# A fused patch, fast-weight attention and mixture-of-experts kernel: the down weights of the experts are loaded and split before the attention loop instead of in it

## The reference

```python
h = patch_norm_linear(x)                      # 32 images, 36 patches each, 3840 features -> 192
h = concatenate([h, txt], axis=1)             # 32 x 164 tokens of 192
n = layernorm(h)
# fast weights: k0, v0, g0 come from batch 0 alone
retrieved[t] = q[t] @ fw[t];  fw[t+1] = 0.95 * fw[t] + 0.1 * g0[t] * outer(k0[t], v0[t])   # per head, 8 heads of 64
h = h + n + retrieved @ w_out.T
n = layernorm(h);  xf = rms_norm(n, norm_w)
probs = softmax(xf @ router_w.T);  comb = probs * one_hot(top_k(probs, 2))               # 8 experts
y = einsum(silu(xf @ gate_w[e].T) * (xf @ up_w[e].T) * comb[:, e], down_w[e])             # 384 hidden
out = h + n + y
```

## Time and profile before

| | |
|---|---|
| time, median of three runs | 548.85 us (548.56 to 549.72) |
| the profiled execution: span | 547.2 us; the page gives no other time of this execution |
| busy: TensorE / weight loads / VectorE / ScalarE / GpSimd | 89% / 84% / 69% / 56% / 35% |
| mean granted TensorE clock | 0.962 of full |
| head, attention loop, experts | up to 111 us, 111 to 224 us, 236 to 547 us |

### The profile page before, as it was taken

One profiled execution on the slowest core, in us unless ns is written; L12 is line 12 of the kernel. 1 busy time (PEld: TensorE's weight loads), 2 busy tenths in 40 slices (PEclk: granted clock), 3 DMA queues, 4 the chain that ended last, 5 costly groups with the idle time before them and its releaser, 6 DMA issues.

```text
span 547.2 us, 12568 instructions
## 1 busy us (share of the span) xinstructions
PE 484.7 (89%) x3157; PEld 461.4 (84%) x3158; DVE 375.3 (69%) x1293; ACT 304.8 (56%) x773; POOL 192.3 (35%) x272
## 2 busy tenths in 40 slices
PE   2999998998798987789999999999999999999900
PEld 2999997887576876789999999999999999999800
DVE  4969996459789879848566566565565565565597
ACT  5485967449578876435444444444444444444473
POOL 1000000006577777733333333333433433433330
PEclk9999999999799989799999999999999999999965
DMA  8988214711433342542222222222222222235897
GB/s 322 415 331 350 63 53 130 283 38 51 120 94 110 101 126 76 139 117 73 71 76 76 68 79 73 68 82 70 68 83 69 69 83 68 68 84 145 273 353 223
DMA packets 62463, 71.67 MB, mean 131 GB/s; under 512 B 19057, under 2 KB 56626, under 8 KB 61410
## 3 DMA queue, kind: packets, MB, share of 16 engines
q1 hardware_dynamic: 49920, 51.43, 30.6%
q0 software_dynamic: 8208, 16.95, 8.7%
q10 hardware_dynamic: 4306, 2.95, 1.8%
HBM read 49.43 MB, written 21.86 MB: 130 GB/s over the span
## 4 chain that ended last, share of the span: by engine, by line
PE 71%; DVE 15%; DMA 6%; ACT 4%; issue 2%; ACTq 1%; SPq 0%; POOL 0%; DVEq 0%; POOLq 0%
PE bank L838 8%; PE pair L838 6%; PE bank L1088 5%; PE bank L1084 5%; PE bank L1087 5%; PE bank L1086 5%; PE bank L1085 5%; PE bank L1095 5%; PE pair L1104 4%; PE bank L1104 4%; PE pair L1073 3%; PE pair L983 3%; ACT yall L749 2%; PE pair L987 2%; PE pair L1106 2%
## 5 line engine op out<-in xcount | busy, mean ns | idle before, releaser
L782 POOL DMA_INDIRECT disp<-xf,posu x82 | 85.0, 1037 | 151.0 <-ACT xf L654 123.8
L1575 DVE TENSOR_TENSOR hh<-sg,bank 128x384 f32<-128x384 f32 x89 | 49.3, 554 | 99.5 <-ACT sg L730 99.5
L812 POOL DMA_INDIRECT ydram<-ysb,dnow x89 | 88.5, 994 | 69.4 <-DMA ydram<-ysb,dnow 35.1
L730 ACT ACTIVATE sg<-bank 128x384 f32<-128x384 f32 x89 | 43.7, 492 | 116.8 <-PE bank L1088 116.8
L1084 PE MATMUL bank<-wa,xh 128*128 x178 | 67.5, 379 | 0.0
L1088 PE MATMUL bank<-wa,xl 128*128 x178 | 60.4, 339 | 0.0
L1087 PE MATMUL bank<-wa,xh 128*128 x178 | 59.9, 337 | 0.0
L1085 PE MATMUL bank<-wa,xh 128*128 x178 | 59.7, 336 | 0.0
L1086 PE MATMUL bank<-wa,xl 128*128 x178 | 59.7, 335 | 0.0
L809 POOL COPY dnow<-dest 128x1 uint32 (+1 forms) x89 | 16.9, 190 | 114.2 <-DVE ysb L1585 104.8
L838 PE MATMUL bank<-wcT,imgT 128*128 128x193 f32 x240 | 41.7, 335 | 10.6 <-DMA imgT<-in_pixels 10.6
(11 more groups left out here) (262 smaller groups left out, 1171.2 us busy)
## 6 DMA issues: line engine op xcount, KB each, us to landing
xs<-disp SPq DMA_DIRECT2D x89, 96.0 KB, 2.0
band<-in_bands SPq DMA_DIRECT2D x4, 1536.0 KB, 12.1
yall<-ydram SPq DMA_DIRECT2D x7, 768.0 KB, 7.8
imgT<-in_pixels SPq DMA_DIRECT2D x4, 768.0 KB, 12.5
imgT<-in_pixels SPq DMA_DIRECT2D x2, 1536.0 KB, 16.0
hres<-in_text SPq DMA_DIRECT2D x1, 3072.0 KB, 25.5
wa<-in_gate_up_w SPq DMA_DIRECT2D x8, 384.0 KB, 8.5
ring<-in_gate_up_w SPq DMA_DIRECT2D x32, 96.0 KB
```

Of the source, the lines that this page charges most:

```text
L782: pool.indirect_dma_start(disp, bass.IndirectOffsetOnAxis(ap=posu[c % XBUF][:, 2 * j + k:2 * j + k + 1], axis=0), xfd[c % XBUF][:, j, :], None
L812: pool.indirect_dma_start(ydram, bass.IndirectOffsetOnAxis(ap=dnow[b][:], axis=0), ysb[r][:], None).then_inc(s_ys[b], 16)
```

## The change

The load of the down weights moves up in SP's order, behind that of the attention weights and behind a wait for the row sums. Units 0 to 3 leave the loop: `down_high` and `down_low` do them at four places of the head in ScalarE and three in VectorE (two pieces at one of them). `turn_units` deals only the other 24 units over the same 19 turns.

```diff
         def turn_units(t):
 
-            return range(min(t, TURNS) * UNITS // TURNS, min(t + 1, TURNS) * UNITS // TURNS)
+            n = UNITS - DOWN_UNITS
+            return range(DOWN_UNITS + min(t, TURNS) * n // TURNS, DOWN_UNITS + min(t + 1, TURNS) * n // TURNS)
...
                     sp.dma_start(aw[:], attn_w).then_inc(s_attw, 16)
+                    sp.wait_ge(s_red, 2)
+                    sp.dma_start(wd4[:, :, 1, :].bitcast(F32), down_w).then_inc(s_rawd, 16)
 
             sp.wait_ge(s_sq, 30)
             sp.wait_ge(s_pat, PTILES)
-            sp.dma_start(wd4[:, :, 1, :].bitcast(F32), down_w).then_inc(s_rawd, 16)
...
+            def down_high(n):
+                if n == 0:
+                    act.wait_ge(s_rawd, 16)
+                g = slice(6 * n, 6 * n + 6)
+                nc.scalar.copy(wd4[:, g, 0, :], wd4[:, g, 1, :].bitcast(F32)).then_inc(s_hi, 1)
...
                     for n in range(4):
                         projection(n)
                     add_norm(3, slice(4, 8))
+                    down_high(0)
...
             add_norm(4)
+            down_high(1)
+            down_high(2)
             act.wait_ge(s_k0, 5)
...
             add_norm(5)
+            down_high(3)
             act.wait_ge(s_gs, 1)
...
+            def down_low(n):
+                v.wait_ge(s_hi, n + 1)
+                raw = wd4[:, 6 * n:6 * n + 6, 1, :]
+                v.tensor_tensor(raw, raw.bitcast(F32), wd4[:, 6 * n:6 * n + 6, 0, :].bitcast(F32), ALU.subtract
+                                ).then_inc(s_lo, 1)
...
             for h in range(4):
                 vals(h)
+            down_low(0)
+            down_low(1)
             v.wait_ge(s_k0, 6)
...
             v.tensor_tensor(kgate[:], kgate[:], cst[:, C_KEY:C_KEY + CHUNKS], ALU.mult).then_inc(s_kgr, 1)
+            down_low(2)
...
             v.memset(bank[4][0:DH, 0:2 * XC], 0.0).then_inc(s_st0, 1)
+            down_low(3)
             st.wait()
```

More of the change, by code:

```diff
@@ L379, in unit @@
             k = n - DOWN_UNITS
-            return None if k < 0 else (k // 3, k % 3)
+            return k // 3, k % 3
         def turn_units(t):
-            return range(min(t, TURNS) * UNITS // TURNS, min(t + 1, TURNS) * UNITS // TURNS)
+            n = UNITS - DOWN_UNITS
+            return range(DOWN_UNITS + min(t, TURNS) * n // TURNS, DOWN_UNITS + min(t + 1, TURNS) * n // TURNS)
         def load_results(eng, g):
@@ L666, in high @@
             def high(n):
[L667 to L671, removed]
-                else:
[L673 to L680, removed]
+                e, k = unit(n)
+                if k == 0:
+                    act.wait_ge(s_rawm[e], 16)
+                    ins = nc.scalar.activation(wa5[:, e, 0], wa5[:, e, 1].bitcast(F32), ACT.Copy, scale=nwab[:, 0:1])
+                else:
+                    r = 2 * e + k - 1
+                    act.wait_ge(s_rawr[r % RING], 32 * (r // RING + 1))
+                    ins = nc.scalar.activation(wa5[:, e, 2, k - 1], ring[r % RING][:], ACT.Copy, scale=nwab[:, 1:2])
                 ins.then_inc(s_hi, 1)
@@ L1435, in low @@
                 v.wait_ge(s_hi, n + 1)
-                if unit(n) is None:
-                    raw = wd4[:, 6 * n:6 * n + 6, 1, :]
-                    ins = v.tensor_tensor(raw, raw.bitcast(F32), wd4[:, 6 * n:6 * n + 6, 0, :].bitcast(F32), ALU.subtract)
-                else:
[L1440 to L1448, removed]
+                e, k = unit(n)
+                if k == 0:
+                    raw = wa5[:, e, 1]
+                    ins = v.scalar_tensor_tensor(out=raw, in0=raw.bitcast(F32), scalar=nwab[:, 0:1],
+                                                 in1=wa5[:, e, 0].bitcast(F32), op0=ALU.mult, op1=ALU.subtract)
+                else:
+                    both = wa5[64:P, e, 2, k - 1, :]
+                    ins = v.scalar_tensor_tensor(out=both, in0=ring[(2 * e + k - 1) % RING][64:P, :], scalar=nwab[64:P, 1:2],
+                                                 in1=both.bitcast(F32), op0=ALU.mult, op1=ALU.subtract)
                 ins.then_inc(s_lo, 1)
```

## The result

| | before | changed |
|---|---|---|
| time, median | 549.29 us (548.56 to 550.14, 4 runs) | 544.91 us (543.73 to 545.99, 4 runs) |
| ratio, 95% interval | | 0.9921 (0.9902 to 0.9941) |
| profiled execution | span 547.2 us | span 544.2 us, own time 545.99 us |
| mean granted TensorE clock | 0.962 | 0.969 |

The forecast was 544.6 us. Two later sets of runs of the changed kernel, each beside the kernel before on its chip, gave 545.22 us (541.67 to 548.46, 12 runs; 0.9919, 0.9895 to 0.9944) and 544.38 us (542.31 to 544.59, 6 runs; 0.9919, 0.9896 to 0.9942). The gain is 4.4 us. Of the times further down one, e7's of 553.67 us, is a slow execution, which the ratios leave out.

What follows compares the result with a forecast made beforehand. It took VectorE and TensorE taking turns in the attention loop as the bound, with GpSimd's scatter queue as second chain. 0.2 + 0.3 + 2.0 + 1.7 = 4.2 us off the 548.85 us median gave 544.6 us, range 542.2 to 547.4.

Steps and rivals of the forecast that it cites:

- Transfer: Down load on SyncE's queue, moved behind the attention weights: lands near 61 us in a 10 us hole, gains nothing.
- Head: Four down pieces placed in idle time of ScalarE and VectorE before the loop: cost nothing.
- The rival of a load in the way: SyncE's queue at 64.78: the down load delays the fourth band, making the kernel slower, up to 551.1 us; chance 0.05.
- Before residual 1: Loop, VectorE: a rest piece replaces a down piece ahead of these residuals; saves 0 to 0.7 us, taken as 0.2.
- ScalarE's deviations: Loop, chunk 1: ScalarE casts fewer down pieces, so VectorE's 0.28 us wait for the deviations goes; saves 0.3 us.
- the row of pieces: VectorE before residual 2, from 133.09 us: pieces in a row shrink from 4.78 to 2.82 us; saves 2.0 us.
- The clock: TensorE's half-clock falls in chunks 3 and 8: one of two goes, at the dear price; saves 1.7 us, between 0 and 4.7.
- GpSimd's cap: GpSimd's scatter queue in the loop allows 3.2 to 9.6 us of gain, likely 5.5; binds only where no fall comes.
- my sign of being wrong: Loop's end: the prediction is wrong if GpSimd's last loop scatter moves less than the mask of chunk 10.
- The stretches: Scatters on GpSimd lengthened beyond their regular steps, 6.3 us in all; estimated to shrink to 4 us.
- The hole at the experts' start: TensorE idles between fillers and first expert slot as VectorE outgains GpSimd; a fall there costs 1.7 to 3.0 us; chance 0.08.
- the rival of no fall: Loop: both clock falls go, 7.2 us on VectorE's chain, cut to about 6 by GpSimd, 542.9 us; chance 0.22.

Runs made afterwards that it cites:

- e7: Changed kernel with 4 filler products on TensorE ahead of each mask wait from chunk 2 on; 546.19 us, ratio 0.9912 to the kernel before.
- e1: Kernel before with only the down load moved behind the attention weights, all splits still in the loop; 550.02 us, ratio 1.0012.
- e3: Changed kernel with ScalarE's casts in the head but VectorE's four down subtractions back in the loop; 548.75 us, ratio 0.9981.
- e4: Changed kernel with the 24 remaining units at the turns they had among 28; 546.48 us, ratio 0.9946.
- e9: Kernel before with 4 filler products ahead of each mask from chunk 2 on; 550.45 us, ratio 1.0007.
- a0_after: The changed kernel run again, unaltered, beside the kernel before; 545.22 us over 12 runs, ratio 0.9919.
- r_e8: Changed kernel with 4 fillers ahead of each mask from chunk 2 on and 54 instead of 40 before the experts; 543.83 us, ratio 0.9915.
- r_after: The changed kernel run again, unaltered, on the same chip as r_e8; 544.38 us over 6 runs, ratio 0.9919.
- e2: Changed kernel with each head piece done twice on ScalarE and VectorE; 552.51 us, ratio 1.0064.

## Why the prediction was right, and which of its terms were not

**Transfer, nothing: right** (e1). Its size was off: I took 410 GB/s, and once the down load ran alone it moved at 325 to 353, so it landed at 62.9 and not 61. That left 2.9 us to the band's issue.

**Head, nothing: right**, with the waits left that I had worked out, to 0.2 us. The rival of a load in the way, my only slower one, has nothing for it.

**Before residual 1, 0.2 us: zero.** Mask 0 to mask 2 is 19.46 before and 19.45 after. VectorE waits 0.56 us for TensorE at 126.95. The measured value is the lower bound of my 0 to 0.7; I should have taken it, since I had written that TensorE leads there.

**ScalarE's deviations, 0.3 us, and the row of pieces, 2.0 us: 0.46 and 2.1.** Together 2.56 for my 2.3, and e3 separates them. e4 shows why it is no more than that.

**The clock, 1.7 us: this is the term that was mis-sized.** I had one of two falls stay "at the dear price". The dear one went, mask 3 to mask 4 fell from 12.99 to 9.90 us, a gain of 3.1; the cheap one stayed at its price (mask 4 to mask 10: 59.8 and 59.7 us). Against the profile before, the loop gained 2.56 + 3.1 + 0.1 = 5.8 us, not 4.2. But the profile before was not typical. In e1, e3 and e9, where the pieces' row still stands, the fall behind mask 3 holds 3.4 us and not 6.9, so that mask 3 to mask 4 is 11.45 to 11.57 us and the fall costs 1.5 to 1.7; and the late fall does not come (mask 4 to mask 10: 58.2 to 58.3 us). The changed kernel's three profiles have the late one and not the first. Either side then has one fall of 3.4 us, the clock term is about nothing, and on VectorE's chain, mask 0 to mask 10, 101.6 to 102.1 us stand against 99.3 to 99.7: 1.9 to 2.7 us, the pieces and little more.

The medians lie 4.4 us apart all the same, and the ledger shows where the rest can be. In e1, e3 and e9 GpSimd's queue leads at the loop's end: it stood still for 3.16 to 3.28 us behind chunk 1, while chunk 2 was late, and waited for no row after that. Its last scatter came 112.7, 113.6 and 114.1 us after mask 0, against 109.0 to 109.4 in the changed kernel. Between the profiles nearest the medians (e3 and e9 against a0_after) that is 4.2 to 4.7 us. So there the pieces' row is still the cause, but the gain reaches the experts through the queue that I had called a cap, and which I had said to bind only where no fall comes. The figure of the forecast came out right partly by luck: it was added up on VectorE's chain, with a clock term from one profile that had lost more than most. This reading rests on a few profiles; I ran nothing that tests it by itself.

**GpSimd's cap, likely 5.5 us: right in size**, against the profile before. Standstill and stretches came to 5.7 us, first scatter to last, and the last scatter moved by 5.7 counted from mask 0 (mask 10 by 5.8: my sign of being wrong, that the scatter moves less than the mask, was met by 0.03 us, which says nothing). That the cap binds was only argued until r_e8 gave 1.4 us on VectorE's chain and 0.3 on GpSimd's. The stretches, which I had put at 4 us, were 3.5. The longest, 1.71 us, is at 143.53, and the row of VectorE that runs then is the main piece of chunk 3, from 143.41, a `scalar_tensor_tensor` on two SBUF inputs. By the inference in the Trainium skill (SBUF — State Buffer, Who interferes with whom), which is for `tensor_tensor` and for the writing of descriptors alone, the 1.92 us beside a down piece should not have come from that writing. The stretches did shrink when the pieces left, from 6.3 to 3.5 us (4.1 in a0_after), but no run here stretches a scatter by that one cause alone, nor tells which part of a scatter is held up.

**The hole at the experts' start, 0.08: the mechanism came, in some executions.** The wait was 2.44 us and the fall behind it cost 2.6, as I had priced it (1.7 to 3.0), while I had given the case as one in which VectorE gains more than GpSimd. They gained alike (5.8 and 5.7). What opened the hole in the changed kernel's profile, and not in the one before, is the length of the same 80 filler products: 9.18 us, all at full clock, in place of 11.87, part of them at half. In a0_after and r_after a fall over the fillers makes them 10.81 us long, they reach 1.6 us nearer to the slot, and none comes behind it. A warm-up counted in products is shortest just when the clock is high, and then it covers least; I had taken its end for fixed. My own mechanism, the two chains drifting apart, shows in other profiles: in e3 and e9 the fillers were 12.0 us long, yet the slot came 2.22 and 1.98 us behind them, since GpSimd's queue led, and a fall of 3.4 us followed that cost 1.6. So the hole is no invention of the change; versions with the old row of pieces have it too. The mean granted clock of each run points the same way without a profile. In a0_after the four runs at 0.971 took 541.67 to 544.81 us, the two at 0.960 and 0.963 took 547.77 and 548.46. Falls are part of what makes one execution of this kernel differ from the next; the four at 0.971 are still 3.1 us apart.

**What stays open** is what decides whether a fall comes. Waits of 1.61 and 1.64 us ahead of mask 3 went either way. So did those of 1.73 and 1.74 us ahead of masks 8 and 9: a fall behind four of ten. My argument against the rival of no fall, that 1.9 us is longer than the 1.73 that brought one, had no more to stand on than that.

## What to carry to other kernels

Before work is moved out of a busy stretch, ask which engine leads once it is gone: here all four subtractions left VectorE's loop, 5.3 us of work, and before the clock's share what came of it on that chain was 2.1 us, its excess over TensorE in one chunk. Then ask which queue caps the gain or carries it, and count it from its own timeline; here GpSimd's, idle 0.3 us at a time, had no slack. And price a fall of the clock over several profiles, since one row of work lost 1.5 to 1.7 us to it in three profiles and 3.1 us in a fourth.

## What was unexpected of the hardware

- **A wait of 2 us ahead of a stretch of work, and the clock.** Of 14 profiles, five had 1.98 to 3.53 us of idle TensorE ahead of the first slot, and in all five the clock fell behind it and the time from the first slot to the end was 312.8 to 314.4 us. Nine had 0 to 1.46 us, none fell, and it was 311.1 to 311.7. Nothing between was seen there. In the loop the waits part less well: behind 2.01 us it fell in three of three profiles, behind 1.73 to 1.74 us in four of ten cases, behind 1.83 us (e2) not, and behind 1.54 us in changed and r_after but not in e1, e3 and e4.
- **A fall can come with no idle time in front.** In e4 the clock fell at 102 us, in a head whose code is that of the changed kernel, and in e2 at 103, and from 97 us on neither timeline shows TensorE idle before it; the last waits before, ending at 94 and 95 us, were 0.95 and 0.93 us, as in the changed kernel (0.95), which had no fall there.
- **Half clock can last long.** It held for 3.4 us in most falls of the loop and 6.9 in one; at the experts' start for 3.4 (e3, e9) or 6.8 (changed, e4, e2); and for 20 in e2's head.
- **One load alone ran slower than several.** 2.36 MB moved at 325 to 353 GB/s on their own, against 355 to 448 while other loads were in flight.
